# One product instruction per state in place of two, in the second pass of a Mamba block on one Trainium2 core

## The reference

```python
x = x + 0.5 * ffn(layernorm(x), ffn_weight, ffn_bias)       # ternary weight, scaled
x = x + mamba(layernorm(x), ...)
x = x + 0.5 * ffn(layernorm(x), ffn_weight, ffn_bias)

def mamba(x):
    u, z = split(x @ W_in.T, 2)
    u = silu(causal_conv4(u))
    dt_r, Bm, Cm = split(u @ W_xproj.T)                     # Bm, Cm: 16 states a token
    dt = softplus(dt_r @ W_dt.T + b_dt)
    dA  = exp(dt[..., None] * A)                            # [token, 1024, 16]
    dBu = dt[..., None] * Bm[:, :, None, :] * u[..., None]  # the product of this case
    h_t = dA_t * h_(t-1) + dBu_t;   y_t = sum_n h_t * C_t
    return ((y + u * Dskip) * silu(z)) @ W_out.T
```

## Time and profile before

| | before |
|---|---|
| time, median of 3 runs | 2961.16 us (2957.45 to 3604.93) |
| span of the profiled execution | 2958.3 us, 37688 instructions |
| DVE busy | 2378.5 us (80%) |
| PE busy | 2439.5 us (82%) |
| ACT busy | 2024.5 us (68%) |
| POOL busy | 1874.5 us (63%) |
| product instructions L1064 | 512, together 1231.8 us |
| scans L1268 | 1024, together 1187.8 us |

### The profile page before, as it was taken

One profiled execution on the slowest core, in us unless ns is written; L12 is line 12 of the kernel. 1 busy time (PEld: TensorE's weight loads), 2 busy tenths in 40 slices (PEclk: granted clock), 3 DMA queues, 4 the chain that ended last, 5 costly groups with the idle time before them and its releaser, 6 DMA issues.

```text
span 2958.3 us, 37688 instructions
## 1 busy us (share of the span) xinstructions
PE 2439.5 (82%) x12448; PEld 1400.3 (47%) x12448; DVE 2378.5 (80%) x3197; ACT 2024.5 (68%) x3520; POOL 1874.5 (63%) x1673
## 2 busy tenths in 40 slices
PE   3577998998998736788888888888888889888897
PEld 1233444444443315555555555555555555555553
DVE  5566667677666649999999999999999999999992
ACT  2233766666766767778777777778777777777783
POOL 1112222222221138989989989989989989899991
PEclk8778999999999857889989999999989999999999
DMA  6454233233332256675675775676666766766744
GB/s 206 165 199 165 92 129 121 94 129 114 101 129 105 82 201 157 150 175 123 168 179 115 171 172 124 168 169 131 170 160 133 172 149 150 168 140 157 170 98 100
DMA packets 200290, 429.26 MB, mean 145 GB/s; under 512 B 44512, under 2 KB 93920, under 8 KB 199840
## 3 DMA queue, kind: packets, MB, share of 16 engines
q1 hardware_dynamic: 160928, 284.23, 29.1%
q0 software_dynamic: 39168, 142.62, 25.5%
HBM read 190.86 MB, written 110.10 MB: 102 GB/s over the span
## 4 chain that ended last, share of the span: by engine, by line
DVE 36%; PE 9%; ACT 7%; issue 6%; POOL 4%; DMA 1%; SPq 0%; DVEq 0%; POOLq 0%; ACTq 0%
DVE h L1268 25%; DVE y L1281 7%; PE p_g L1406 4%; POOL dbu L1064 3%; ACT p_da L1156 3%; PE p_ht L1372 2%; ACT tokt L1186 1%; ACT tokt L1193 1%; DVE x L1305 1%; PE p_g L1389 1%; ACT y_part L1173 1%; DVE q L1294 1%; DVE small L55 1%; DVE o L1315 1%; PE p_g L1415 1%
## 5 line engine op out<-in xcount | busy, mean ns | idle before, releaser
L1268 DVE TENSOR_TENSOR_SCAN h<-p_da,dbu 128x512 f32<-128x512 f32 x1024 | 1187.8, 1206 | 135.5 <-ACT p_da L1156 110.6
L1064 POOL TENSOR_TENSOR dbu<-dtu_,bb 128x1024 f32<-128x1024 f32 x512 | 1231.8, 2494 | 21.5 <-DMA dtu_<-dtu_scratch 20.9
L1156 ACT ACTIVATE p_da<-dt_,neg_a 128x255 f32<-128x255 f32 x2048 | 882.1, 467 | 331.8 <-DVE h L1268 325.9
L1372 PE MATMUL p_ht<-ident,h 128*128 128x128 f32 x4096 | 575.0, 300 | 131.5 <-DVE h L1268 128.6
L1372 PEld LDWEIGHTS p_ht<-ident,h 128*128 128x128 f32 x4096 | 520.6, 156 | 220.5 <-DVE h L1268 197.3
L714 PE MATMUL p_u<-xz,wu 128*128 128x512 f16 x1536 | 349.2, 385 | 8.2 <-DVE xz L508 6.2
L1406 PE MATMUL p_g<-wo,tokt 128*128 128x512 f16 x1536 | 350.7, 386 | 1.6 <-ACT tokt L1193 1.6
L1281 DVE SCALAR_TENSOR_TENSOR y<-p_ht,ct,y 128x1024 f32<-128x1024 f32 x272 | 344.3, 1266 | 8.0 <-PE p_ht L1372 7.7
L1415 PE MATMUL p_g<-wz,xz 128*128 128x512 f16 x1536 | 346.4, 382 | 0.0
L70 POOL TENSOR_TENSOR small<-small,consts 128x1 f32<-128x1 f32 x96 | 68.8, 717 | 423.9 <-DVE small L63 423.9
L363 POOL TENSOR_TENSOR late<-dt,u 128x512 f32<-128x512 f32 x64 | 81.6, 1274 | 376.9 <-DVE dt L561 376.9
(11 more groups left out here) (117 smaller groups left out, 2862.0 us busy)
## 6 DMA issues: line engine op xcount, KB each, us to landing
y<-y_part POOLq DMA_DIRECT2D x224, 512.0 KB, 5.8
bb<-b_scratch SPq DMA_DIRECT2D x128, 256.0 KB, 3.6
xin<-in_x SPq DMA_DIRECT2D x32, 512.0 KB, 5.8
x_scratch<-x SPq DMA_DIRECT2D x32, 512.0 KB, 5.1
xz_scratch<-xz SPq DMA_DIRECT2D x16, 1024.0 KB, 6.2
y_scratch<-late SPq DMA_DIRECT2D x32, 512.0 KB, 5.4
dt_scratch<-dt SPq DMA_DIRECT2D x64, 256.0 KB, 2.1
dtu_scratch<-late SPq DMA_DIRECT2D x64, 256.0 KB, 2.4
```

The source lines that it names most:

```text
L1064: nc.gpsimd.tensor_tensor(state[:, 4 * f:4 * f + 4, :], dtu[:, 4 * f:4 * f + 4, :], bb[n // NB % 2][:, n % NB:n % NB + 1, :].to_broadcast( ...
L1156: ins_ = nc.scalar.activation(p_da[p % 2][:, k * T2 + 1:(k + 1) * T2], dt[:, g, 1:], ACT.Exp, scale=neg_a[:, g, n:n + 1])
L1268: nc.vector.tensor_tensor_scan(h[n % 2][:, 2 * p:2 * p + 2, :].rearrange("p g t -> p (g t)"), p_da[p % 2][:], dbu[n % 2][:, 2 * p:2 * p + ...
L1372: mm = nc.tensor.transpose(p_ht[t][:, g * P:(g + 1) * P], h[n % 2][:, g, t * P:(t + 1) * P], ident[:])
```

## The change

In `times_b` the product of one state is one instruction over all eight groups (128x2048) where it was two over four groups (128x1024). The semaphore `product_done` goes up by 1 a state and no longer by 2. In the first slot of a chunk this one instruction waits for both loads of `dtu`. Both loads of the next chunk wait for the whole product of state 15.

```diff
 def load_dtu(c, f):
     if not (isinstance(c, int) and c == 0):
-        wait_alone(sp, product_done, ((c - 1) * NS + NS - 1) * 2 + f + 1)
+        wait_alone(sp, product_done, c * NS)
     sp.dma_start(dtu[:, 4 * f:4 * f + 4, :], dram["dtu"][bass.ds(c, 1), :, 4 * f:4 * f + 4].rearrange(
         "c p g t -> p (c g) t")).then_inc(dtu_loaded[f], 16)
...
                 state = dbu[n % 2]
-                for f in range(2):
-                    if n == 0:
+                if n == 0:
+                    for f in range(2):
                         wait(pool, dtu_loaded[f], i * 16 + 16)
-                    wait(pool, scan_done, i * (NS * 4) + (n - 2) * 4 + 2 * f + 2)
-                    nc.gpsimd.tensor_tensor(state[:, 4 * f:4 * f + 4, :], dtu[:, 4 * f:4 * f + 4, :],
-                                            bb[n // NB % 2][:, n % NB:n % NB + 1, :].to_broadcast([P, G // 2, T2]),
-                                            ALU.mult).then_inc(product_done, 1)
-                wait(pool, product_done, (i * NS + n + 1) * 2)
+                wait(pool, scan_done, i * (NS * 4) + (n - 2) * 4 + 4)
+                nc.gpsimd.tensor_tensor(state[:], dtu[:], bb[n // NB % 2][:, n % NB:n % NB + 1, :].to_broadcast([P, G, T2]),
+                                        ALU.mult).then_inc(product_done, 1)
+                wait(pool, product_done, i * NS + n + 1)
                 wait(pool, carry_done, (i - 1) * NS + n + 1)
                 nc.gpsimd.tensor_tensor(state[:, :, 0], state[:, :, 0], carry[:, n, :], ALU.add).then_inc(dbu_done, 1)
```

## The result

The changed kernel takes 2996.31 us (median of 4 runs, 2990.45 to 2998.75) where the kernel before takes 2961.16: a ratio of 1.0117, 95% interval 1.0102 to 1.0132. (The 2961.16 is the median of three runs, 2957.45 to 2964.59; a fourth run of the kernel before, a slow one of 3604.93 us, is left out.) It is slower by about 35 us, within 2% and above the range of 2957 to 2992 that was forecast. The profiled execution has a span of 2993.3 us, 35.0 us more than before.

The account below looks back on a forecast made before the run. DVE, with its waits for ACT, was taken as the bound, POOL just in front. -1.4 (first chunk) + 2.4 (first boundary) + 8.4 (14 boundaries) = +9.4 us on the 2958.3 us span, plus 2.9 to the median: 2970 us, range 2957 to 2992.

Parts of the forecast that it names:

- POOL is not the bound, and its 44 us bring nothing: Over 256 states POOL's saved 44 us go almost all into its waits; rival, POOL the bound: 2917 us, chance 0.03.
- The long product does not hold DVE: DVE's scans beside POOL's product: term zero; rival, DVE held: 276 us more, 3237 us, chance 0.01.
- The gain of 1.4 us in the first chunk: First chunk: seven products in a row save 0.17 us each, plus 0.2 us for the very first: -1.4 us.
- One product is 4.50 us: One 128x2048 instruction on POOL takes 4.50 us where two take 4.67; rival, nothing saved: 2987 us, chance 0.10.
- The whole product stands behind the second landing, and this is the price: Chunk boundary: all 4.50 us of product lie behind the second dtu landing, where 2.34 do now; 14 boundaries cost 8.4 us.
- Step 1: Chunk boundary near 1990 us: the product of state 15 ends 0.34 us earlier, at 1982.48 for 1982.82.
- Step 3: Same boundary: second half of dtu lands 5.5 us after its issue, at 1988.3; ends 5.2 and 8.6.
- Step 4: Same boundary: product runs from 1988.4 to 1992.9, POOL 1.9 us late at state 0, under the margin of 3.0.
- Steps 5 to 7, the margins: States 1 to 3: POOL 1.75, 0.83, 0.66 us late; margin 0.12 at state 3, so DVE starts 0.54 us late.
- The first boundary, 2.4 us: First chunk boundary, DVE already waiting for POOL: product ends 2.9 us later, less three states of 0.17: 2.4 us.
- The cost of `dt` behind `dtu`, put at nothing: SP's queue: four dt loads issued when they are now, any lateness mostly beside POOL's own: nothing.
- The rival of a late pair: Boundaries: accumulating DMA beside the dtu loads, landing 8.6 us: 53 us, 3014 us; chance 0.10, of which 0.03 past 2%.

Follow-up runs that it names:

- e3: Changed kernel with only the product of state 15 split again, the product of state 0 still waiting for both loads of dtu: 2975.91 us, ratio to before 1.0046.
- e4: Changed kernel with the accumulating DMA of state 12 issued before the product of state 15 and not after it: 2994.80 us, ratio to before 1.0115.
- e6: Changed kernel with one load of dtu of 1 MB in place of two of 512 KB: 2980.62 us, ratio to before 1.0068.
- e7: Changed kernel with 60 more transposes on PE at the start of the second pass, shifting its instruction fetches: 2995.55 us, ratio to before 1.0109.
- e1: Changed kernel with the products of states 15 and 0 split again, each dtu load waiting for its own half: 2961.97 us, ratio to before 1.0000.
- e2: Changed kernel with only the product of state 0 split again, both dtu loads still after the whole product of state 15: 2967.47 us, ratio 1.0017.

## Why the prediction was wrong

**Where the time is.** The span grew by 35.0 us. The first boundary's share is 5.7 us: from the first scan of the first chunk to that of the second it is 107.4 us for 101.7. The next 14 chunk starts drift apart by 25.2 us, 1.8 us each. The last chunk and the start add 1.9 us. The remaining 2.3 us lie behind the last scan, where no product is left: PE's same 254 matmuls take 57.48 us at a granted clock of 0.91 and not 55.07 at 0.93. By windows over the tail, before and changed kernel (PE busy first, clock third from the end):

```profile
2888.00:2958.00 70.00, 55.07 (x254) 27.34 (x254) 16.23 (x36) 20.17 (x30) 10.88 (x13) 0.93 0.42 96
```

```profile
2921.00:2993.00 72.00, 57.48 (x254) 27.79 (x254) 16.06 (x36) 20.06 (x30) 10.81 (x13) 0.91 0.41 94
```

The profiled executions of e3, e4, e6 and e7 have such a tail, too (70.2 to 70.5 us behind the last scan), and those of e1 and e2 that of the kernel before (67.8 for 68.1). No experiment here was about it, and why it is so stays open.

**Step by step.**

- *POOL is not the bound, and its 44 us bring nothing.* Right: e1 has 224 wide products and the time of before. The saving in the group of the products is 41 us.
- *The long product does not hold DVE.* Right: the scans take 1195 to 1226 ns beside the wide products, 1193 to 1226 before.
- *The gain of 1.4 us in the first chunk.* From its first scan to the end of its last the first chunk takes 98.6 us for 100.6, so it gained 2.0 us. In e1 it is 0.6 us, and the next chunk starts 1.2 us later after the first scan than in the kernel before, so no gain is left there.
- *One product is 4.50 us.* Right. View by source line of the changed kernel, min/median/max:

```profile
L1064 POOL TENSOR_TENSOR dbu<-dtu_,bb x256: 4495/4537/5218, 1097.4 to 2911.3; 128x2048 f32<-128x2048 f32 x128
```

- *The whole product stands behind the second landing, and this is the price.* Right in kind: e3 alone costs 13.5 us.
- *Step 1, the product of state 15 ends 0.34 us earlier.* It ends 0.24 us earlier, by the median against ACT's first decay.
- *Step 3, the landing: 5.5 us after the second issue, between 5.2 and 8.6.* This is the step that failed. The median is 6.2 us, 5.4 to 6.5 at 13 of 15 boundaries and 9.2 and 9.9 at two. The forecast took the mean of two pairs of `y` loads, 5.8 and 5.2 us. But the earlier trace rows have 5.8 us for the second load of `dtu` alone, at this very boundary and beside the same accumulating DMA, and the median of the kernel before is 5.6 us; with another 512 KB issued 0.36 us in front, a value under both needed a reason, and the forecast gave none. The pair with 5.2 us does have its accumulating DMA where it is here, about 0.5 us behind the first load, so the `y` rows alone could not show the error. What they lack are the four loads of `dt` right behind; no run parts these from the rest. e4 shows that the accumulating DMA, which the forecast took to be harmless when issued behind the pair, costs 1.3 us all the same.
- *Step 4* left out that POOL starts 0.22 us after the landing where it started 0.07 us after it. With steps 1 and 3 this makes POOL 3.3 us late at state 0 for 1.9.
- *Steps 5 to 7, the margins.* Right, and they are what turned this into 25 us. The forecast stood exactly on the margin of state 1 and 0.5 us over that of state 3, and from there every microsecond of lateness is one of time. It had 0.6 us a boundary for 1.9 us of lateness; with 3.3 us the same steps give 2.0 us a boundary, 28 us over 14, where 25.2 were measured. DVE's waits at the later states stayed as they were, so its lateness is not made up, as the forecast had it. The margins also order the variants: e2 with 1.5 us late costs 5 us, e3 with 2.3 us 13.5, e6 with 2.5 us 19, e4 with 3.0 us 32.
- *The first boundary, 2.4 us.* DVE's wait before the first scan of the second chunk is 8.8 us for 1.1: it costs 7.7 us, and less the 2.0 us gained inside the first chunk these are the 5.7 us above. Its second load took 9.9 us, 3.7 us over the median.
- *The cost of `dt` behind `dtu`, put at nothing.* No run here parts it from the rest; ACT's decays were not what DVE waited for at states 1 and 3.
- *The rival of a late pair* named the accumulating DMA and a landing of 8.6 us at all boundaries. The mechanism is real (e4), at 1.3 and not 3.1 us, and the case of 9 us exists at two boundaries for another reason. The range was too narrow, since it left this rival outside, although between 5.5 and 8.6 us each step of 0.1 us is 1.4 us of time. At 6.2 us the forecast's own sum gives 2981 us. The range would have had to reach about 3000.

**What makes up the difference**, as an estimate from the figures above: 0.7 us more for the landing and 0.25 us more in steps 1 and 4, at 15 boundaries, are 14.3 us; the two slow landings are 6.7 us; the last chunk and the start are 1.9 us and the tail 2.3 us. Together they are 25.2 us, and 2970.6 + 25.2 = 2995.8 us, where 2996.31 were measured. The mechanism of the forecast was right, and the mis-sized term is the landing: its median and the two slow cases together are 17.2 of the 25.2 us.

No variant was faster than the kernel before. The best, e1, is equal to it.

## What to carry to other kernels

Two instructions over the halves of a tile with one buffer are also two points at which the buffer comes free and two at which new data can be used; joining them delays the first half's load by half of the work and puts the whole instruction behind the last landing. The saving of 0.17 us an instruction is small beside that. When an engine runs close behind the bound, write down its margin at each step: below the margin lateness is free, above it each microsecond counts in full, so two delays that cost 5 and 14 us alone cost 34 together here. And when the forecast sits on such an edge, the range has to take in what the uncertain term does beyond it.

## What the runs showed of the hardware

A 16 KB fetch of PE's instructions that starts about half a microsecond before the second of two back-to-back 512 KB loads is issued goes with a landing of 9.2 to 9.9 us in place of 6.2; moving the fetches by adding instructions to PE moved the slow landing to another boundary. Fetches that started at least 1.4 us before the second load, or within 0.3 us of it in e4 and e6, had no landing over 6.6 us. One load of 1 MB (6.1 us) was there before the second of two loads of 512 KB issued 0.36 us apart (6.2 us after its own issue, 6.6 us after the first), and the waiting instruction on POOL started 0.12 us after the landing with one load to wait for and 0.22 us after it with two.
